# Row 0 of a two-layer graph kernel: a third transposed buffer, hand-over by blocks, products of zeros, constants prepared in pieces, and an epilogue product in three fp32r parts

## The chip, the cores and the metric

The kernel runs on one core of one Trainium2 chip. Its engines are TensorE (PE in the profile; its weight loads are PEld), VectorE (DVE), ScalarE (ACT), GpSimd (POOL) and SyncE (SP, which here only issues transfers). Sixteen DMA engines move data between HBM and the on-chip memory. The metric is the time of one execution in microseconds (us), lower is better.

## The reference

Two graph layers with a dense 6144 x 6144 matrix `adj` and features `x` of 6144 x 128, each followed by a residual and a normalisation. Cut to what matters:

```
x_norm = layernorm(x, g_in, b_in)
gate   = hard two-way choice from x_norm @ Wn + bn + gumbel(u)          # one number per node
view2  = (adj * gate[:, None] * gate[None, :]) @ x_norm
fg     = sigmoid(concat([x_norm, view2]) @ Wg + bg)
fused  = fg * (x_norm @ W1 + b1) + (1 - fg) * (view2 @ W2 + b2)
x      = layernorm(x + layernorm(fused + x, g_out, b_out))              # first layer
mv     = tanh(|x W^T| / |x| * artanh |x|) * (x W^T) / |x W^T|, clipped to a ball
xt     = logmap0(mobius_add(mv, expmap0(bias)))                         # features of the second layer
h      = expmap0(relu(logmap0(expmap0(adj @ xt))))                      # with clips to the ball
out    = layernorm(x + h)
```

## The kernel before

**Tiles.** Nodes are taken in 12 chunks of 512 (`NCH`, 4 blocks of 128, `BLK`). `adj` comes as 144 tiles of 1 MB, tile (c, q) being what output row c takes from chunk q. A tile n has two halves m = 2n and 2n + 1. A ring `A` holds five tiles. TensorE multiplies in fp32r, which keeps only part of the mantissa, so each half (128x1024) is split in two: ACT writes the high part (L565, `split_high`), DVE subtracts it from the half and writes the low part (L761, `split_low`), and PE makes three products for each of two blocks, high by high, low by high and high by low (L1023 to L1025). The places for split halves are four ring slots and some room in features not yet made (`XTH`, `XTL`), eight at this point.

**Row 0 is different.** Output row 0 (tiles 0 to 11) is summed while the features are made. PE multiplies the unsplit tile by unsplit features `FULL` in plain fp32 (L1021). For each chunk k, PE, ACT and DVE hand over in a ring: ACT `normalize` (L528, four blocks into `YB`), PE `transposes` (L1008), ACT `transposed` (L538, into one of two buffers `XNTB` = `XNT`, `X1T`, then a store to HBM by the ACT queue), PE `rows_and_logits` (L1015), DVE `gate_begin` (three small operations), ACT `gate_exp`, DVE `gate_end` (six small operations, L744 to L749), ACT `gated` (L550, four blocks into `FULL`), ACT `gated_high` (L556) and DVE `gated_low` (L753), which make the split features `XGH` and `XGL`. ACT's program is, for k = 0, 1, ...: `transposed(k+2)`, `gated(k+1)`, store of k+2, `normalize(k+3)`, `gated_high(k)`, load of block k+6 of x, `gate_exp(k+2)`. DVE's is: small step of k+3 (L719), `gate_end(k+1)`, `stats_pre(k+4)` (L710 to L716, which waits for block k+4 of x), `gate_begin(k+2)`, `gated_low(k)`. After its last `gated_low`, DVE runs `prepare()`: weights scaled, four bias vectors split in three bf16 terms (L766 to L777). ACT copies `RM` (L692) and only then begins to split tile 12.

**Epilogues.** Row c's sum is finished by an epilogue, front c, spread over the halves of the next row by tables: event e of row c + 1 is done after half 24(c + 1) + number, where the first number of a pair holds for the rows up to `LATE` = 6 and the second for later ones. For front 0, DVE's event "gate" (L853) stands after half 28, PE's "l0" (L1104 to L1112) after half 27. "gate" waits for three transfers that SP's `load_front` issues (`GB`, the gates for 512 nodes, `XNT` and `XR`; the semaphore `epi_in` counts all three). "l0" makes, for each of four blocks, a bias product, `XNT` by `RX` (256 columns, fp32, L1108), for the first fronts `XR` by the identity (L1110), and `GB` by `RS` (L1112). Then ACT takes tanh (L627), DVE fuses (L860 on) and normalises, with POOL for the powers. At the end SP stores the row (`store_x1`), and SP loads no tile meanwhile, as it runs in order.

**SP's order.** Tile n is loaded once tile n - 5 has been split (in row 0: used by PE). Before tile 16 stands the store of the gates to HBM, after `gate_rows` (L611 on ACT). Before tile 17 stands a wait for that store's landing, then `load_front(0)`.

Of the kernel before, what the change touches and what calls it, by code (L numbers as in the profile page):

```python
# [11 lines left out]
P = 128  # L12
BLK = 4
# [62 lines left out]
DVE_FIRST = {"m2m": (6, 1), "part": (7, 3), "gate": (4, 1), "q": (7, 1), "fuse": (10, 6), "stats1": (10, 8),  # L76
# [3 lines left out]
ACT_FIRST = {"mx": (3, 1), "tq": (9, 3), "tanh": (10, 6), "y1": (13, 11), "x1": (19, 15), "x1t": (19, 21),  # L80
# [28 lines left out]
def build(nc, x, adjT, u, w1, b1, w2, b2, wg, bg, wn, bn, g_in, b_in, g_out, b_out, w_hyp, b_hyp, out):  # L109
# [29 lines left out]
    with ExitStack() as ctx:  # L139
# [6 lines left out]
        FULL = sb("FULL", [P, 3, CW])  # L146
# [19 lines left out]
        RX = sb("RX", [P, 2 * P])  # L166
# [10 lines left out]
        BR = sb("BR", [P, CW], BF16)  # L177
# [5 lines left out]
        WH = PART[:, 1, 0:P]  # L183

# [34 lines left out]
        for name in (  # L219
# [4 lines left out]
                "xnt_stored0", "xnt_stored1", "epi_in",  # L224
                "hb_sq", "hb_norm", "hb_tanh", "hb_ready", "y2_ready", "rm_psum", "rm_ready", "wt_scaled", "bias_ready",
# [44 lines left out]
        XNTB = (XNT, X1T)  # L270
# [32 lines left out]
        def whole(q):  # L303
            return FULL[:, q % 3, :]

# [29 lines left out]
        def _(sp):  # L335
# [54 lines left out]
            for n in range(NCH + 3, NT):  # L390
# [4 lines left out]
                if n == 17:  # L395
                    sp.wait_ge(S["gate_stored"], 16)
                    sp.wait_ge(S["xnt_stored0"], 16 * (NCH // 2))
                    sp.wait_ge(S["xnt_stored1"], 16 * (NCH // 2))
                    load_front(0)
# [105 lines left out]
        def _(act):  # L505
# [18 lines left out]
            def normalize(k):  # L524
                act.wait_ge(S["pre_nm"], k + 1)
                wait_n(act, "pre_tr", k - 1)
                for t in range(BLK):
                    last = a.activation(YB[k % 2][:, blk(t)], XIN[k % 3][:, blk(t)], ACT.Identity,  # L528
                                        bias=NMP[:, k % 3, t:t + 1], scale=RSP[:, k % 3, t:t + 1])
                last.then_inc(S["pre_y"], 1)  # L530

            def transposed(k):
# [3 lines left out]
                wait_n(act, "pre_x", k - 1)  # L536
                wait_n(act, f"xnt_stored{k % 2}", 16 * (k // 2))
                a.activation(XNTB[k % 2][:, :], tbank(k), ACT.Identity, bias=BINC[:, 0:1],  # L538
# [6 lines left out]
            def gated(k):  # L545
# [3 lines left out]
                for t in range(BLK):  # L549
                    last = a.activation(whole(k)[:, blk(t)], xcell(k, t)[:, 0:P], ACT.Copy,  # L550
                                        scale=GATE[:, k * BLK + t:k * BLK + t + 1])
                last.then_inc(S["xgf"], 1)

            def gated_high(k):
                act.wait_ge(S["xgf"], k + 1)
# [147 lines left out]
        def _(dve):  # L703
# [23 lines left out]
            def neg_mean_pre(k):  # L727
                dve.wait_ge(S["pre_rs"], k + 1)
                wait_n(dve, "pre_y", k - 2)
# [454 lines left out]
```

## Time and profile before

| | us |
|---|---|
| median of three runs | 959.79 (958.04 to 961.10) |
| the profiled execution's own time | 959.55 |
| its span in the trace | 957.8 |
| PE busy | 911.9 (95%) |
| DVE busy | 788.0 (82%) |
| ACT busy | 680.3 (71%) |
| POOL busy | 232.4 (24%) |

The span is the stretch that the trace covers; 1.75 us of the execution's time lie around it. Busy time is the sum over an engine's instructions. PE's ends are modelled, and a matmul's busy time overlaps the next one's, so what a matmul costs in a row of them is read from start to start.

### The profile page before, as it was taken

The numbers are of one execution on the slowest core, as the hardware profiler recorded it, in microseconds if no ns is written. First come the engines' busy times: TensorE is split into PE (matmuls) and PEld (weight loads), VectorE is DVE, ScalarE is ACT, GpSimd is POOL, SyncE is SP. The second block draws the span as 40 slices with busy tenths as digits, with TensorE's granted clock in tenths as the row PEclk, the third lists the DMA queues.
The fourth block names the chain that finished last, engine by engine and source line by source line (L and its number), as shares of the span: only waits on it lengthen the run. The fifth ranks groups of instructions, "written<-read, shape, count | busy, mean of one in ns | idle before, by whom it ended". The sixth has DMA issues, their size and how long they took to land.

```text
span 957.8 us, 12537 instructions
## 1 busy us (share of the span) xinstructions
PE 911.9 (95%) x4032; PEld 720.3 (75%) x4032; DVE 788.0 (82%) x1781; ACT 680.3 (71%) x1214; POOL 232.4 (24%) x201
## 2 busy tenths in 40 slices
PE   4998998999999999999999999998999999999993
PEld 3555776777888878888888888886777878778772
DVE  3658899999989799879686775869899898989886
ACT  4786687878767576757566465666878989789873
POOL 2220212111111121101020010201100764485473
PEclk9999999999999999999999999999999999999997
DMA  7978596876949486958666584566799999999980
GB/s 264 358 282 314 224 424 250 327 316 254 380 192 386 185 350 224 346 190 284 232 253 230 177 304 179 216 258 229 275 355 363 410 375 408 371 402 394 419 333 33
DMA packets 51825, 281.72 MB, mean 294 GB/s; under 512 B 6528, under 2 KB 8496, under 8 KB 20656
## 3 DMA queue, kind: packets, MB, share of 16 engines
q1 hardware_dynamic: 46432, 271.48, 73.8%
q10 hardware_dynamic: 5328, 9.44, 2.8%
q8 instruction: 32, 0.52, 0.2%
q14 instruction: 33, 0.27, 0.1%
HBM read 271.44 MB, written 9.46 MB: 293 GB/s over the span
## 4 chain that ended last, share of the span: by engine, by line
PE 59%; DVE 24%; POOL 5%; ACT 5%; DMA 3%; issue 3%; POOLq 0%; DVEq 0%; SPq 0%; ACTq 0%
PE PS L1023 17%; PE PS L1025 17%; PE PS L1024 17%; DVE AL L761 5%; DVE XGL L761 4%; DVE XTL L761 3%; POOL r_rs L456 2%; PE PS L1112 2%; PE PS L1108 2%; DVE BS L710 2%; PE PS L1021 1%; DMA FU<-in_x_dram 1%; DMA A<-in_adjT_dram 1%; ACT FULL L550 1%; PE PS L1122 1%
## 5 line engine op out<-in xcount | busy, mean ns | idle before, releaser
L565 ACT ACTIVATE AH<-A 128x1024 fp32r<-128x1024 f32 x247 | 252.7, 1057 | 114.1 <-PE PS L1025 92.5
L761 DVE TENSOR_TENSOR AL<-A,AH 128x1024 fp32r<-128x1024 f32 x247 | 294.2, 1218 | 40.6 <-ACT AH L565 39.4
L1023 PE MATMUL PS<-AH,XGH 128*128 128x512 f32 x344 | 139.0, 404 | 4.0 <-DVE AL L761 4.0
L1025 PE MATMUL PS<-AH,XGL 128*128 128x512 f32 x344 | 134.2, 390 | 0.0
L761 DVE TENSOR_TENSOR XGL<-A,XGH 128x1024 fp32r<-128x1024 f32 x113 | 132.2, 1218 | 2.2 <-ACT XGH L565 2.0
L1024 PE MATMUL PS<-AL,XGH 128*128 128x512 f32 x344 | 134.0, 389 | 0.0
L565 ACT ACTIVATE XGH<-A 128x1024 fp32r<-128x1024 f32 x113 | 112.9, 1055 | 13.0 <-DMA A<-in_adjT_dram 11.4
L1023 PE MATMUL PS<-AH,XTH 128*128 128x512 f32 x290 | 114.8, 396 | 3.9 <-DVE AL L761 3.9
L1025 PE MATMUL PS<-AH,XTL 128*128 128x512 f32 x290 | 113.2, 390 | 0.0
L1024 PE MATMUL PS<-AL,XTH 128*128 128x512 f32 x290 | 113.0, 390 | 0.0
L456 POOL TENSOR_TENSOR r_rs<-r_v,NHALF 128x4 f32<-128x4 f32 x24 | 44.4, 1849 | 275.4 <-DVE r_v L716 275.4
L761 DVE TENSOR_TENSOR XTL<-A,XTH 128x1024 fp32r<-128x1024 f32 x92 | 108.5, 1218 | 0.1
L565 ACT ACTIVATE XTH<-A 128x1024 fp32r<-128x1024 f32 x92 | 93.2, 1051 | 6.9 <-DMA A<-in_adjT_dram 3.5
L1023 PE MATMUL PS<-XGH,XTH 128*128 128x512 f32 x226 | 91.3, 404 | 3.6 <-DVE XGL L761 3.6
L1025 PE MATMUL PS<-XGH,XTL 128*128 128x512 f32 x226 | 88.6, 392 | 0.0
L1024 PE MATMUL PS<-XGL,XTH 128*128 128x512 f32 x226 | 88.5, 392 | 0.0
L1023 PEld LDWEIGHTS PS<-AH,XGH 128*128 128x128 f32 x344 | 64.7, 188 | 18.6 <-DVE AL L761 4.3
L1023 PE MATMUL PS<-XTH,XGH 128*128 128x512 f32 x184 | 72.4, 394 | 4.4 <-DVE XTL L761 4.4
L1025 PEld LDWEIGHTS PS<-AH,XGL 128*128 128x128 f32 x344 | 64.6, 188 | 13.9
L1024 PEld LDWEIGHTS PS<-AL,XGH 128*128 128x128 f32 x344 | 64.7, 188 | 13.0
L1025 PE MATMUL PS<-XTH,XGL 128*128 128x512 f32 x184 | 72.3, 393 | 0.0
L1024 PE MATMUL PS<-XTL,XGH 128*128 128x512 f32 x184 | 72.3, 393 | 0.0
(245 smaller groups left out, 1560.2 us busy)
## 6 DMA issues: line engine op xcount, KB each, us to landing
A<-in_adjT_dram SPq DMA_DIRECT2D x243, 1024.0 KB, 7.1
GB<-gate_scratch SPq DMA_DIRECT2D x12, 256.0 KB, 3.6
XNT<-xnt_scratch SPq DMA_DIRECT2D x12, 256.0 KB, 4.0
XR<-in_x_dram SPq DMA_DIRECT2D x12, 256.0 KB, 4.8
x_scratch<-X SPq DMA_DIRECT2D x12, 256.0 KB, 7.7
xnt_scratch<-XNT ACTq DMA_DIRECT2D x6, 256.0 KB, 4.9
xnt_scratch<-X1T ACTq DMA_DIRECT2D x6, 256.0 KB, 3.9
XR<-in_x_dram ACTq DMA_DIRECT2D x4, 256.0 KB, 6.6
```

The lines of the kernel that those rows point to most:

```text
L456: g.tensor_tensor(dst, src, NHALF[:, 0:src.shape[-1]], ALU.pow).then_inc(S[done], 1)
L550: last = a.activation(whole(k)[:, blk(t)], xcell(k, t)[:, 0:P], ACT.Copy, scale=GATE[:, k * BLK + t:k * BLK + t + 1])
L565: a.activation(high(m), A[:, n % RING, h * HW:(h + 1) * HW], ACT.Copy).then_inc(S["hi"], 1)
L710: last = v.bn_stats(BS[:, t, :], src[:, blk(t)])
L761: v.tensor_tensor(low(m), A[:, n % RING, h * HW:(h + 1) * HW], high(m).bitcast(F32), ALU.subtract).then_inc(S["lo"], 1)
L1021: return p.matmul(acc, whole(q)[:, blk(t)], A[:, m // 2 % RING, t * CW:(t + 1) * CW], start=start, stop=stop)
L1023: p.matmul(acc, hi[:, st], high(m)[:, mv], start=start, stop=False)
L1024: p.matmul(acc, hi[:, st], low(m)[:, mv], start=False, stop=False)
L1025: return p.matmul(acc, lo[:, st], high(m)[:, mv], start=False, stop=stop)
L1108: p.matmul(E[:, t, 0:2 * P], XNT[:, blk(t)], RX[:, :], start=False, stop=False)
L1112: last = p.matmul(E[:, t, right], GB[:, blk(t)], RS[:, right], start=False, stop=True)
L1122: last = p.matmul(E[:, t, 0:P + 1], X1T[:, blk(t)], RM[:, :], start=True, stop=True)
```

## The change

Six things are changed.

1. A third buffer, `HY`, joins `XNTB`, with a third store semaphore; `transposed(k)` waits for what used the buffer three chunks ago instead of two.
2. Hand-over by blocks: `pre_y` and `xgf` are raised after each of the four blocks, PE's transposes and row 0's products wait for their own block.
3. Products of zeros: PE multiplies `ones` by the zeroed `BP` (bf16, 512 columns, into a bank that row 1 starts afresh), 16 times at the start and 3 times after each of the first four steps.
4. `prepare()` is cut in pieces, run in the loop over k at k = 6 to 10, between `stats_pre(k+4)` and `gate_begin(k+2)`. The copy of `RM` on ACT moves behind the second half of tile 12.
5. The product `XNT` by `RX` is made in three fp32r parts: `XNH` by `RXH`, `XNL` by `RXH`, `XNH` by `RXL`. For it ACT copies `XNT` to `XNH` (event "xnh": after half 24c + 2, later rows 24c + 0) and DVE subtracts (event "xnl": after half 24c + 3, later rows 24c + 0). For front 0 the copy also waits for the end of row 0, whose `FULL` it overlays. "xnh" waits for `epi_in`, and "l0" for `xnl`. `RX` is split once, in the last piece of the constants.
6. Room: `FULL`'s third buffer becomes `FULL2`; `XNH`, `XNL` and `RXL` lie on what row 0 leaves free.

```
-ACT_FIRST = {"mx": (3, 1), ...
+ACT_FIRST = {"xnh": (2, 0), "mx": (3, 1), ...
-DVE_FIRST = {"m2m": (6, 1), ...
+DVE_FIRST = {"xnl": (3, 0), "m2m": (6, 1), ...
-        XNTB = (XNT, X1T)
+        XNTB = (XNT, X1T, HY)
...
             def transposed(k):
                 act.wait_ge(S["pre_tr"], k + 1)
-                wait_n(act, "pre_x", k - 1)
-                wait_n(act, f"xnt_stored{k % 2}", 16 * (k // 2))
+                wait_n(act, "pre_x", k - 2)
+                wait_n(act, f"xnt_stored{k % 3}", 16 * (k // 3))
...
+                if event == "xnh" and front is not None:
+                    act.wait_ge(S["epi_in"], 48 * (front + 1))
+                    if front == 0:
+                        act.wait_ge(S["used"], 2 * NCH)
+                        act.wait_ge(S["xgl"], NCH)
+                    else:
+                        act.wait_ge(S["l0_mm"], front)
+                    a.activation(XNH[:, :], XNT[:, :], ACT.Copy).then_inc(S["xnh"], 1)
...
-            act.wait_ge(S["rm_psum"], 1)
-            a.activation(RM[:, :], PS[:, 4, 0:P + 1], ACT.Copy).then_inc(S["rm_ready"], 1)
...
+                if m == 2 * NCH + 1:
+                    act.wait_ge(S["rm_psum"], 1)
+                    a.activation(RM[:, :], PS[:, 4, 0:P + 1], ACT.Copy).then_inc(S["rm_ready"], 1)
...
+                if event == "xnl" and front is not None:
+                    dve.wait_ge(S["xnh"], front + 1)
+                    v.tensor_tensor(XNL[:, :], XNT[:, :], XNH[:, :].bitcast(F32), ALU.subtract).then_inc(S["xnl"], 1)
...
+            def keep_clock(count):
+                for _ in range(count):
+                    p.matmul(PS[:, 1, :], ones[:, :], BP[:, :], start=True, stop=True)
...
                 for t in range(BLK):
+                    pe.wait_ge(S["pre_y"], BLK * k + t + 1)
                     last = p.transpose(tbank(k)[:, blk(t)], YB[k % 2][:, blk(t)], ident)
...
                 for t in (2 * h, 2 * h + 1):
+                    if c == 0 and n < N2:
+                        pe.wait_ge(S["xgf"], BLK * q + t + 1)
...
+            pe.wait_ge(S["const"], 1)
+            keep_clock(16)
...
+                    pe.wait_ge(S["xnl"], front + 1)
...
-                        p.matmul(E[:, t, 0:2 * P], XNT[:, blk(t)], RX[:, :], start=False, stop=False)
+                        p.matmul(E[:, t, 0:2 * P], XNH[:, blk(t)], RXH[:, :], start=False, stop=False)
+                        p.matmul(E[:, t, 0:2 * P], XNL[:, blk(t)], RXH[:, :], start=False, stop=False)
+                        p.matmul(E[:, t, 0:2 * P], XNH[:, blk(t)], RXL[:, :], start=False, stop=False)
```

Where instructions move: ACT at the end of row 0 and the start of row 1. Before, `GATET`, then `RM`, then eleven splits in a row up to the tanh of front 0 (an instruction that writes `XTH` or `AH` from `A` is a split).

```order
L556 ACTIVATE XGH<-FULL 128x512 x2
L611 ACTIVATE GATET<-PS 48x128
L692 ACTIVATE RM<-PS 128x129
L565 ACTIVATE XTH<-A 128x1024 x4
L565 ACTIVATE AH<-A 128x1024 x4
```

The same place now:

```order
L559 ACTIVATE XGH<-FULL 128x512 x2
L614 ACTIVATE GATET<-PS 48x128
L568 ACTIVATE XTH<-A 128x1024 x2
L708 ACTIVATE RM<-PS 128x129
L568 ACTIVATE XTH<-A 128x1024
L625 ACTIVATE XNH<-XNT 128x512
L568 ACTIVATE XTH<-A 128x1024
L568 ACTIVATE AH<-A 128x1024 x4
```

`RM` has moved behind two splits, and `XNH` stands behind the third split of row 1, with all others behind it.

DVE at the same place. Before, the constants stand between the last low part of the features and the first low part of tile 12:

```order
L753 TENSOR_TENSOR XGL<-FULL,XGH 128x512 x2
L766 TENSOR_SCALAR RX<-RX 128x128
L767 TENSOR_SCALAR RS<-RS 128x128
L770 TENSOR_TENSOR PART<-PART 128x128
L771 TENSOR_SCALAR PART<-PART 128x128
L772 TENSOR_SCALAR PART<-PART 128x128
L774 CAST BP<-PART 1x512
L775 CAST BR<-PART 128x512
L776 TENSOR_TENSOR PART<-PART,BR 128x512
L774 CAST BP<-PART 1x512
...
L761 TENSOR_TENSOR XTL<-A,XTH 128x1024 x4
```

The same place now:

```order
L761 TENSOR_TENSOR GATE<-TOP,LG 128x4
L794 CAST BP<-PART 1x512
L795 CAST RXH<-PART 128x256
L796 TENSOR_TENSOR RXL<-PART,RXH 128x256
L765 TENSOR_TENSOR XGL<-FULL,XGH 128x512 x2
L773 TENSOR_TENSOR XTL<-A,XTH 128x1024 x4
L871 TENSOR_TENSOR XNL<-XNT,XNH 128x512
L773 TENSOR_TENSOR AL<-A,AH 128x1024
L875 TENSOR_TENSOR GB<-PS,GB 128x512
```

The low parts of row 1 follow the features at once, and `XNL` stands between the fourth and the fifth of them, ahead of the gate.

## Rows read from the trace of the kernel before

**Rows 1.** The page: the chain that ended last, by engine.

```profile
PE 59%; DVE 24%; POOL 5%; ACT 5%; DMA 3%; issue 3%; POOLq 0%; DVEq 0%; SPq 0%; ACTq 0%
```

**Rows 2.** Windows: stretch, length, PE, PEld, DVE, ACT, POOL busy; clock; DMA share, GB/s.

```profile
80.00:90.00 10.00, 6.42 (x21) 5.03 (x21) 9.07 (x12) 8.36 (x9) 0.00 (x0) 0.83 0.86 303
```

**Rows 3.** Timeline, one chunk of row 0: start, length, engine, line, what [idle before].

```profile
61.30 0.37 ACT L550 ACTIVATE FULL<-PS,GATE 128x128 f32<-128x128 f32 x1 [0.66 <-DVE GATE L749]
...
62.31 1.65 ACT L528 ACTIVATE TH<-FU,NMP,RSP 128x128 f32<-128x128 f32 x4
...
63.85 0.63 ACT L556 ACTIVATE XGH<-FULL 128x512 fp32r<-128x512 f32 x1
...
64.51 0.69 DVE L753 TENSOR_TENSOR XGL<-FULL,XGH 128x512 fp32r<-128x512 f32 x1 [1.31 <-ACT XGH L556]
...
65.19 0.16 DVE L744 TENSOR_TENSOR SM<-LG 128x4 f32<-128x4 f32 x1
...
66.39 0.37 ACT L550 ACTIVATE FULL<-PS,GATE 128x128 f32<-128x128 f32 x1 [0.66 <-DVE GATE L749]
...
67.58 0.30 PEld L1021 LDWEIGHTS PS<-A,FULL 128*128 128x128 f32 x2 [0.25 <-ACT FULL L550]
```

**Rows 4.** The start: a piece of the chain, then two rows of the timeline.

```profile
13.52 13.12 DMA FU<-in_x_dram
```

```profile
23.68 0.78 ACT L538 ACTIVATE XNT<-PS,BINC,GINC 128x512 f32<-128x512 f32 x1 [5.42 <-DMA xnt_scratch<-XNT]
...
26.66 0.87 DVE L710 BATCH_NORM_STATS2 BS<-FU 128x6 f32<-128x128 f32 x4 [6.94 <-DMA FU<-in_x_dram]
```

**Rows 5.** Timeline, from row 0 to row 1, ACT, DVE and PE.

```profile
76.98 0.27 ACT L611 ACTIVATE GATET<-PS 48x128 f32<-48x128 f32 x1
...
77.83 0.22 DVE L766 TENSOR_SCALAR RX<-RX 128x128 f32<-128x128 f32 x1
...
78.22 1.96 PE L1021 MATMUL PS<-A,FULL 128*128 128x512 f32 x4
...
78.57 3.88 ACT L565 ACTIVATE XTH<-A 128x1024 fp32r<-128x1024 f32 x4
...
82.39 4.63 DVE L761 TENSOR_TENSOR XTL<-A,XTH 128x1024 fp32r<-128x1024 f32 x4
...
83.76 0.47 PE L1023 MATMUL PS<-XTH,XGH 128*128 128x512 f32 x1 [3.58 <-DVE XTL L761]
...
87.44 0.43 PE L1023 MATMUL PS<-XTH,XGH 128*128 128x512 f32 x1
```

**Rows 6.** Timeline, the transfers that front 0 needs, and DVE's wait for them.

```profile
77.28 0.34 SPq L394 DMA_DIRECT2D gate_scratch<-GATET  x1
...
80.21 0.34 SPq L344 DMA_DIRECT2D A<-in_adjT_dram  x1
...
82.40 0.33 SPq L349 DMA_DIRECT2D GB<-gate_scratch  x1
...
88.94 0.69 DVE L853 TENSOR_TENSOR GB<-PS,GB 128x512 f32<-128x512 f32 x1 [0.78 <-DMA XR<-in_x_dram]
```

**Rows 7.** Timeline of PE: three starts at full clock, then one block of front 0.

```profile
89.10 0.40 PE L1024 MATMUL PS<-XTL,XGH 128*128 128x512 f32 x1
89.33 0.39 PE L1025 MATMUL PS<-XTH,XGL 128*128 128x512 f32 x1
...
91.10 0.59 PE L1108 MATMUL PS<-RX,XNT 128*128 128x256 f32 x2
91.53 0.38 PE L1110 MATMUL PS<-XR,IW 128*128 128x128 f32 x2
91.75 0.81 PE L1112 MATMUL PS<-RS,GB 128*128 128x384 f32 x2
```

**Rows 8.** The chain that ended last, from 175 to 210 us: start, length, what.

```profile
175.07 0.60 DVE GB L853
...
209.60 0.50 PE PS L1023
```

More of the change, by code:

```diff
@@ L75 @@
 CLOSE = 12
-DVE_FIRST = {"m2m": (6, 1), "part": (7, 3), "gate": (4, 1), "q": (7, 1), "fuse": (10, 6), "stats1": (10, 8),
+DVE_FIRST = {"xnl": (3, 0), "m2m": (6, 1), "part": (7, 3), "gate": (4, 1), "q": (7, 1), "fuse": (10, 6), "stats1": (10, 8),
              "nm1": (11, 9), "resid": (13, 9), "curv0": (14, 4), "affine": (13, 11), "stats2": (13, 11),
@@ L145, in build @@
         AL = sb("AL", [P, SPLITS, HW], F32R)
-        FULL = sb("FULL", [P, 3, CW])
+        with nc.sbuf_tensor("FULL", [P, 2, CW], F32) as FULL, nc.sbuf_tensor("BR", [P, CW], BF16) as BR:
+            pass
+        XNH = sb("XNH", [P, CW], F32R)
+        XNL = sb("XNL", [P, CW], F32R)
+        RXL = sb("RXL", [P, 2 * P], F32R)
+        FULL2 = sb("FULL2", [P, CW])
         XGH = sb("XGH", [P, N], F32R)
@@ L303, in whole @@
         def whole(q):
-            return FULL[:, q % 3, :]
+            return FULL2[:, :] if q % 3 == 2 else FULL[:, q % 3, :]
         def second_features(q):
@@ L396, in _ @@
                     sp.wait_ge(S["gate_stored"], 16)
-                    sp.wait_ge(S["xnt_stored0"], 16 * (NCH // 2))
-                    sp.wait_ge(S["xnt_stored1"], 16 * (NCH // 2))
+                    for i in range(3):
+                        sp.wait_ge(S[f"xnt_stored{i}"], 16 * (NCH // 3))
                     load_front(0)
@@ L527, in normalize @@
                 for t in range(BLK):
[L528 to L530 removed]
+                    a.activation(YB[k % 2][:, blk(t)], XIN[k % 3][:, blk(t)], ACT.Identity,
+                                 bias=NMP[:, k % 3, t:t + 1], scale=RSP[:, k % 3, t:t + 1]).then_inc(S["pre_y"], 1)
             def transposed(k):
@@ L549, in gated @@
                 for t in range(BLK):
-                    last = a.activation(whole(k)[:, blk(t)], xcell(k, t)[:, 0:P], ACT.Copy,
-                                        scale=GATE[:, k * BLK + t:k * BLK + t + 1])
-                last.then_inc(S["xgf"], 1)
+                    a.activation(whole(k)[:, blk(t)], xcell(k, t)[:, 0:P], ACT.Copy,
+                                 scale=GATE[:, k * BLK + t:k * BLK + t + 1]).then_inc(S["xgf"], 1)
             def gated_high(k):
-                act.wait_ge(S["xgf"], k + 1)
+                act.wait_ge(S["xgf"], BLK * (k + 1))
                 a.activation(XGH[:, xcols(k)], whole(k), ACT.Copy).then_inc(S["xgh"], 1)
@@ L805, in _ @@
                     stats_pre(k + 4)
+                prepare(k)
                 if k + 2 < NCH:
@@ L1012, in rows_and_logits @@
                 pe.wait_ge(S["pre_xt"], k + 1)
-                wait_n(pe, "xgf", k - 1)
+                wait_n(pe, "xgf", BLK * (k - 1))
                 for t in range(BLK):
-                    last = p.matmul(xcell(k, t), XNTB[k % 2][:, blk(t)], IW[:, :], start=True, stop=True)
+                    last = p.matmul(xcell(k, t), XNTB[k % 3][:, blk(t)], IW[:, :], start=True, stop=True)
                 last.then_inc(S["pre_x"], 1)
```

58 lines of the change are left out of this document (32 added, 26 removed).

## The prediction

> **What bounds the kernel now.** I read the page's chain first: PE holds 59% of the chain and DVE 24% [rows 1]. Whatever PE neither computes nor waits for is worth nothing, so the question for each edit is whether PE's start on something moves. Then I read three stretches in the timeline.
>
> In row 0 the reader is to see a ring of ACT and DVE that leaves PE out: `gated` starts at 61.30, `normalize` at 62.31, `gated_high` at 63.85, DVE's `gated_low` at 64.51, `gate_end` at 65.19, and the next `gated` at 66.39, 5.09 us after the last [rows 3]. PE waits 0.25 us for `FULL` in such a chunk [rows 3], so it is almost as slow, but the ring sets the pace.
>
> From row 0 to row 1, PE's last products of row 0 begin at 78.22 and last to about 80.2; it then idles 3.58 us until DVE, which spends 77.83 to 82.39 on constants, has the first low part, and starts at 83.76 [rows 5]. The granted clock of that stretch is 0.83 on average [rows 2]: nine products of row 1 run at the lower level (1.2 GHz), from 83.76 to 87.44, 0.41 us each [rows 5], where at the higher one they take 0.23 [rows 7].
>
> Front 0's inputs are the third: the gates are stored from 77.28, the loads wait for that store until 82.40, and DVE's gate starts only at 88.94, let go by the last of the three transfers [rows 6].
>
> **The change part by part.** *Third buffer.* ACT waited 5.42 us for the first store, until 23.68 [rows 4]; that wait goes. What is late next: DVE, in order, stands in `stats_pre(4)` until 26.66 for a block of x that was issued at 13.52 and took 13.12 us [rows 4], and `gate_end(2)`, without which ACT has nothing to go on with, is behind it. ACT issues that load after `gate_exp(0)`, at the same place of its program as before; a warmer PE lets it issue some tenths earlier, behind the same transfers. I take 0 for the start. Bounds: at most the 3 us from 23.68 to 26.66 if the transfer comes so much earlier, and 1 us lost, since PE now stands idle longer before 30 us, goes on at the lower clock, and has only 0.25 us a chunk in which to catch up. I add 0.2 for that.
>
> *Hand-over by blocks.* PE's 0.25 us of waiting a chunk go, but the ring of ACT and DVE has the same links of the same length; nothing comes of it until the last chunk, which no longer depends on the ring: 0.1 us. *Products of zeros.* They lie where PE waits for x and for ACT; 0.
>
> *Constants in pieces.* DVE has 1.31 us idle ahead of each `gated_low` [rows 3], and no `stats_pre` at k of 8 or more. The pieces last 0.4 to 1.6 us (4.56 us in all [rows 5], and the split of `RX`). They hide, but for about 0.5 us at k = 9 on the way to the last gates, which the hand-over by blocks covers for PE, not for the store of the gates. With them out of the way ACT splits from 77.3 (after `GATET` [rows 5]) and DVE from about 78.5, so PE could start row 1 at 80.2 instead of 83.76 and at the higher clock. Alone that is 3.6 us, and 9 x (0.41 - 0.23) = 1.6 us, 5.2 in all.
>
> *The new wait.* It isn't alone. ACT's `XNH` stands behind the third split of row 1 and waits for all three transfers of front 0. They land at 88.9 [rows 6]. Does the change bring them forward? Their loads start at the landing of the gates' store (82.40), whose issue at 77.28 follows `GATET` [rows 6], and `GATET` follows the last gates of the same ring; if anything it is later by up to 0.5 us. So ACT, having made splits 24, 25, 26 by 80.6, stands still until 88.9. Queued behind it are all further splits, behind those DVE and PE:
> - PE has three halves, 6 products of 0.23 us each: 80.2 + 4.1 = 84.3, then idle.
> - `XNH` is 128x512 on ACT, as `gated_high`: 0.6 us [rows 3]. Then split 27 on ACT (3.88 us for four, so 1.0 each [rows 5]), its low part on DVE (4.63 us for four, so 1.16 each [rows 5]) with 0.1 between: 88.9 + 0.6 + 1.0 + 0.1 + 1.2 = 91.8. PE has stood for 7.5 us, over the 3.58 after which the row showed the lower clock.
> - Half 27 at the lower level: 6 x 0.41 = 2.5, to 94.3. DVE meanwhile does `XNL` (as `gated_low`, 0.69 [rows 3]), low part 28 and the gate (0.69 [rows 6]), to 94.3. So l0 of front 0 starts at 94.3, before at about 91.0, a little ahead of its second product at 91.10 [rows 7]: 3.3 late. Its first 1.3 us still run at the lower clock: 0.6 more. Its `RX` part is shorter by 0.3 (below). Front 0's products are done 3.6 us later than before.
>
> From there on DVE is the chain, from the fusing of each front to the next gate, until 209.60 [rows 8]; a delay of front 0 is passed on whole, and the tile loads that wait for its end move with it. With up to 0.5 us for later gates I take +3.8 (3.0 to 4.5).
>
> *Cost of the parts on DVE and ACT.* A `XNL` of 0.7 and a `XNH` of 0.6 in each front. Front 1 falls into a stretch where ACT and DVE wait for tiles now and then: 0.4. Front 2's gate at 175.07 is inside the DVE chain [rows 8]: 0.7. Front 3 comes just behind that stretch: 0.2. Later rows are PE's, and DVE has room. Sum 1.3 (0 to 2.5).
>
> *The product.* Start to start, the fp32 product of 256 columns takes 91.53 - 91.10 = 0.43 us [rows 7]. Three fp32r products of 256 columns are not in the trace; of 512 columns one takes 89.33 - 89.10 = 0.23 [rows 7]. Half of that is 0.115, and a bit for what doesn't halve: 0.12, so 0.36 for three, and 0.07 saved for each block, 0.28 a front. Bounds: no less than 3 x 0.115; at most as long as the 512-column one if the weight load sets the pace, 0.69, a loss of 0.26 a block. Nearest is the 512-column row, which hides the same load; I keep to 0.12. It counts where PE is the chain, fronts 3 to 10: 8 x 0.28 = 2.2 gained (between 2.7 gained and 8.3 lost). That a load of 128 columns can be hidden under 256 columns is what the 128-column product makes likely: 91.75 - 91.53 = 0.22 us for two parts with a load each, 0.11 a part [rows 7].
>
> The Trainium skill (TensorE: Matmul & The Clock Gate, section LDWEIGHTS (loading the stationary operand)) gives a load of 128 columns as 128 / 1.2 = 107 ns, which is as long as 256 columns stream; by it, as an estimate, three parts take 0.32 to 0.33 us and the eight fronts give 3.3 us instead of 2.2. The trace has no such product to agree or disagree.
>
> **Sum.** Against the profiled execution's 959.55: start +0.2, last chunk -0.1, row 1 and front 0 +3.8, parts on DVE and ACT +1.3, product -2.2: +3.0, so 962.55. The median of the runs is 0.24 above the profiled execution: **962.8**. A measurement of this kernel can tell about 0.3% (2.9 us) from no change, that is 956.9 to 962.7, so my time stands right on the upper bound.
>
> **Rivals.**
> - *Faster: the start goes with the third buffer* (0.15). If block 4 of x lands up to 3 us earlier, as the same engines had other work queued then, all of row 0 moves, with the gates and front 0: 962.8 - 3 = 959.8; from there it is decided by the store of the gates: if that store of the gates no longer lands behind a tile, the 5.1 us to its landing (77.28 to 82.40 [rows 6]) shrinks by about 3, and ACT's stand with it: 956.8, and less with a shorter product. Against it: the load is at the same place in ACT's queue.
> - *The stall is there but is absorbed* (0.17): DVE's chain behind front 0 has slack that the rows don't show, for instance as it has fewer halves to split while it waits for tanh. Then front 0's delay counts by a half: 962.8 - 1.9 = about 961.
> - *The parts are slow* (0.10): three loads don't hide, 0.69 for 0.43. Eight fronts at 0.26 x 4 and the 2.2 not gained: 962.8 + 8.3 + 2.2 = 973 at the far end, 967 half way. The deciding point is a start to start of 0.143 us.
> - *The change does all it says* (0.05): the transfers of front 0 land before ACT needs them. 5.2 + 2.2 - 1.3: 953.7. The 88.94 speaks against it.
> - My forecast, the stall passed on whole: 0.53, spread from 961 to 965.5.
>
> The range of 8 in 10 is 956.0 to 967.0, which leaves out the case that does all it says and most of the slow parts. Faster by over 0.3%: half of the first rival and all of the fourth, 0.13. Slower: the slow parts and some 0.30 of my forecast, 0.40. Within: 0.23 of my forecast, the absorbed stall and the other half of the first rival, 0.47.
>
> **What would show it.** In the profile after: ACT idle before `XNH` by some 8 us, let go by the transfer of `XR`; PE idle some 7 us behind the third half of row 1, and nine or so products at half clock after it; front 0's gate at 94 instead of 88.94; start to start of the three parts at 0.12; `gated` every 5.09 us in row 0 as before; block 4 of x at 26 to 27. I am wrong if ACT has no such wait, if the ring's pace changes, or if block 4 lands well ahead of 26 us.

## The result, and the profile after

Times are medians in us over the runs of each kernel; the ratio is after over before, with its 95% interval.

| kernel | runs | median | lowest to highest | profiled execution | its span |
|---|---|---|---|---|---|
| before | 20 | 958.31 | 955.3 to 961.1 | 959.55 | 957.8 |
| after | 20 | 961.86 | 959.43 to 964.06 | 961.41 | 959.6 |

The ratio is 1.0037 [1.0029, 1.0045]: 3.55 us slower. (The first three runs of before had a median of 959.79; over twenty it is 958.31. The prediction's +3.0 was made against the profiled execution, so it is the difference that should be compared: +3.0 forecast, +3.55 measured.)

The page of the kernel after, its first part and its chain of work that ended last. Before, PE had 59% of the chain and DVE 24% [rows 1]:

```profile
PE 914.2 (95%) x4108; PEld 719.0 (75%) x4108; DVE 795.7 (83%) x1795; ACT 684.9 (71%) x1226; POOL 233.5 (24%) x201
...
PE 54%; DVE 28%; POOL 5%; DMA 4%; ACT 4%; issue 3%; POOLq 0%; SPq 0%; ACTq 0%; DVEq 0%
```

DVE has gained what PE lost: a longer part of the span is paced by DVE. Next the timeline of the kernel after from row 0 to front 0 (columns: start us, us busy, engine, line, operation, out<-in, shape, and in brackets the idle time before it and what ended it). First SyncE's queue, then ACT, DVE and PE; it answers to [rows 5 to 7].

```profile
76.69 0.34 SPq L399 DMA_DIRECT2D gate_scratch<-GATET  x1
82.11 0.33 SPq L354 DMA_DIRECT2D GB<-gate_scratch  x1
82.96 0.67 SPq L356 DMA_DIRECT2D XR<-in_x_dram  x1
...
76.40 0.27 ACT L614 ACTIVATE GATET<-PS 48x128 f32<-48x128 f32 x1
78.61 1.06 ACT L568 ACTIVATE XTH<-A 128x1024 fp32r<-128x1024 f32 x1
88.60 0.63 ACT L625 ACTIVATE XNH<-XNT 128x512 fp32r<-128x512 f32 x1 [8.93 <-DMA XR<-in_x_dram]
100.42 0.60 ACT L638 ACTIVATE TH<-PS 128x512 f32<-128x512 f32 x1 [3.61 <-PE PS L1148]
...
77.65 3.50 DVE L773 TENSOR_TENSOR XTL<-A,XTH 128x1024 fp32r<-128x1024 f32 x3 [0.32 <-ACT XTH L568]
90.21 1.23 DVE L773 TENSOR_TENSOR XTL<-A,XTH 128x1024 fp32r<-128x1024 f32 x1 [9.06 <-ACT XTH L568]
93.08 0.68 DVE L875 TENSOR_TENSOR GB<-PS,GB 128x512 f32<-128x512 f32 x1
...
79.02 0.47 PE L1048 MATMUL PS<-XTH,XGH 128*128 128x512 f32 x1 [0.16 <-DVE XTL L773]
91.49 0.79 PE L1048 MATMUL PS<-XTH,XGH 128*128 128x512 f32 x1 [8.11 <-DVE XTL L773]
94.22 0.54 PE L1141 MATMUL PS<-BP,ones 128*128 128x384 bf16 x1
```

PE gets into row 1 at 79.02, where before it started at 83.76 [rows 5], but after three halves it has nothing more: ACT stands for 8.93 us ahead of `XNH` until front 0's `XR` has landed, all further splits are queued behind it, DVE stands 9.06 us for the next split and PE 8.11 us for DVE's low part. Front 0's gate on DVE is at 93.08, before at 88.94 [rows 6]: 4.14 us late. PE starts the products of front 0 (l0) at 94.22, before at 90.93, and ACT's tanh of front 0, which the next steps hang on, comes at 100.42, before at 96.99: 3.43 us late. The rows of before:

```profile
90.93 0.34 PE L1107 MATMUL PS<-BP,ones 128*128 128x384 bf16 x1
...
96.99 0.60 ACT L627 ACTIVATE TH<-PS 128x512 f32<-128x512 f32 x1 [3.78 <-PE PS L1112]
```

Stretches of the kernel after (columns: window, its length, busy time and count of PE, of PE's loads, DVE, ACT, POOL, then granted clock, DMA share, GB/s):

```profile
80.00:90.00 10.00, 3.38 (x15) 2.44 (x13) 1.14 (x2) 1.40 (x2) 0.00 (x0) 0.92 0.85 288
90.00:100.00 10.00, 8.51 (x39) 6.41 (x39) 9.79 (x10) 6.81 (x8) 0.00 (x0) 0.74 0.69 249
```

Over this time DMA goes on at 85% and 69%, DVE and ACT have hardly anything in the first window and DVE is full in the second.

Where the loss comes from, by DVE's gate of each front (start in us, in one profile of each kernel):

| front | 0 | 1 | 2 | 3 | 4 | 5 | 6 | 8 | 10 | 11 | span |
|---|---|---|---|---|---|---|---|---|---|---|---|
| before | 88.94 | 130.92 | 174.99 | 219.07 | 263.15 | 310.59 | 358.44 | 465.21 | 582.86 | 645.95 | 957.8 |
| after | 93.08 | 134.83 | 179.50 | 224.16 | 268.83 | 314.95 | 362.18 | 468.29 | 585.28 | 648.05 | 959.6 |
| difference | 4.14 | 3.91 | 4.51 | 5.09 | 5.68 | 4.36 | 3.74 | 3.08 | 2.42 | 2.10 | 1.8 |

Three things are to be read off it: a delay of 4.1 us arises before front 0's gate (3.4 at its tanh); it grows by 0.6 us in each of the three steps from front 1 to front 4; from there 0.3 to 1.3 us a front come back. (These two profiles differ by 1.8 us, less than the medians do; block 4 of x, for which DVE waits at the start, landed 1.1 us earlier in the one of after, as told below.) The growth is `XNL`: from gate to gate it is 44.67, 44.66 and 44.67 us in after, 44.07, 44.08 and 44.08 in before, and in e2 below, which has no `XNL`, 44.07 in the last two of these steps.

### The profile page after: what moved, and what is told of

It is laid out like the page before. It is cut to its first block, busy times and chain, and to the rows that moved or that the text cites. A ratio compares the mean times of both kernels' runs of the same rounds, so it can differ in the third digit from the quotient of the medians.

```text
span 959.6 us, 12742 instructions
## 1 busy us (share of the span) xinstructions
PE 914.2 (95%) x4108; PEld 719.0 (75%) x4108; DVE 795.7 (83%) x1795; ACT 684.9 (71%) x1226; POOL 233.5 (24%) x201
## 4 chain that ended last, share of the span: by engine, by line
PE 54%; DVE 28%; POOL 5%; DMA 4%; ACT 4%; issue 3%; POOLq 0%; SPq 0%; ACTq 0%; DVEq 0%
PE PS L1048 16%; PE PS L1050 16%; PE PS L1049 16%; DVE AL L773 7%; DVE XTL L773 5%; DVE XGL L773 4%; POOL r_rs L461 3%; PE PS L1046 2%; DVE BS L722 2%; PE PS L1148 1%; DMA FU<-in_x_dram 1%; DMA A<-in_adjT_dram 1%; ACT FULL L554 1%; POOL r_minv L461 1%; ACT X L533 1%
## 5 line engine op out<-in xcount | busy, mean ns | idle before, releaser
L1050 PE MATMUL PS<-XGH,XTL 128*128 128x512 f32 x226 | 88.1, 390 | 0.0
L1049 PE MATMUL PS<-XGL,XTH 128*128 128x512 f32 x226 | 88.1, 390 | 0.0
```

Of the source, the lines that this page charges most:

```text
L1049: p.matmul(acc, hi[:, st], low(m)[:, mv], start=False, stop=False)
L1050: return p.matmul(acc, lo[:, st], high(m)[:, mv], start=False, stop=stop)
```

## The experiments

All kernels below compute the whole reference. The three groups of runs had medians of before of 958.9, 958.5 and 958.9, so only ratios are compared; 0.001 is about 1 us. e10 has five runs, e6 six, e11 seven and e12 eight, the others eleven or twelve. All profiles are of single executions, and one kernel's executions lie 2.5 to 6 us apart. Against before:

| kernel | ratio | interval |
|---|---|---|
| after | 1.0037 | 1.0029 to 1.0045 |
| e1: after, front 0's steps behind half 31 | 0.9993 | 0.9984 to 1.0002 |
| e2: after, product whole | 1.0005 | 0.9994 to 1.0017 |
| e3: before, parts alone | 1.0009 | 1.0000 to 1.0017 |
| e4: before, third buffer alone | 1.0001 | 0.9990 to 1.0012 |
| e5: after, constants in one go | 1.0009 | 0.9999 to 1.0019 |
| e6: after, no products of zeros | 1.0041 | 1.0028 to 1.0054 |
| e7: after, parts from front 5 on | 1.0002 | 0.9992 to 1.0011 |
| e8: e7, front 0's steps behind half 31 | 0.9993 | 0.9982 to 1.0004 |
| e9: e7, inputs of front 0 sooner | 1.0001 | 0.9992 to 1.0010 |
| e10: e9, zeros ahead of front 0 | 0.9959 | 0.9947 to 0.9972 |
| e11: after, zeros inside the stall | 1.0032 | 1.0021 to 1.0043 |
| e12: e9, front 0 two halves later | 0.9971 | 0.9960 to 0.9983 |

**Is it the wait of `XNH`?** e1 keeps every piece of work and moves the four events of front 0 (so far behind halves 26, 27, 28 and 27) behind half 31, so that five more splits stand ahead of the waiting instruction on ACT.

```
+FRONT0 = {"xnh": 7, "xnl": 7, "gate": 7, "l0": 7}
-                    out.setdefault(2 * NCH * c + after[c > LATE], []).append((event, c))
+                    at = FRONT0.get(event, after[0]) if c == 1 else after[c > LATE]
+                    out.setdefault(2 * NCH * c + at, []).append((event, c))
```

> The changed kernel, with front 0's four steps (XNH on ACT, XNL and the gate on DVE, l0 on PE) all placed behind half 31 of row 1, instead of behind 26, 27, 28 and 27. Nothing is computed otherwise. Theory (the wait of ACT for front 0's transfers is what loses the time): all eight places for split halves are filled before ACT waits, so ACT's wait of 8.93 us before XNH shrinks to 2 to 4 us, PE's 8.11 us of idle time in row 1 to under 1.5 us, no product of row 1 runs at the lower clock, front 0 is fused near 97.3 instead of 101.05, and the time is 3.5 to 5 us under the changed kernel's: 957 to 958.4, ratio to the kernel before 0.999 to 1.000. Rival (DVE paces rows 1 to 4 anyway and absorbs the stall): DVE's fuse moves, but the time stays at 961 to 962, ratio 1.003 to 1.004.

Measured: 0.9993, 4.2 us better than after. The timeline of e1:

```profile
89.08 0.63 ACT L627 ACTIVATE XNH<-XNT 128x512 fp32r<-128x512 f32 x1 [4.05 <-DMA XR<-in_x_dram]
91.40 0.32 PE L1143 MATMUL PS<-BP,ones 128*128 128x384 bf16 x1 [0.63 <-DVE GB L877]
97.77 0.69 DVE L884 SCALAR_TENSOR_TENSOR FU<-TH,PS 128x512 f32<-128x512 f32 x1 [3.33 <-ACT TH L640]
110.21 0.76 PE L1050 MATMUL PS<-AH,XGH 128*128 128x512 f32 x1 [2.93 <-DVE AL L775]
```

The transfer lands at about the same time (89.08, in after 88.60, in before 88.94), but ACT has only 4.05 us to wait and PE 0.63. Moving the steps removes the loss. It doesn't turn it into a gain: PE idles 2.93 us before 110.21 instead, when it waits for a low part that DVE makes late, and goes on at the lower clock. A later place alone is worth little: e8 against e7 below, which have no `XNH` there, is 0.9 us, within the noise.

**Is it the product in parts?** e2 is after with one fp32 product from `XNT` and `RX` again, without `XNH` and `XNL`; e3 is the opposite, before with the parts alone.

```
...
-                        p.matmul(E[:, t, 0:2 * P], XNH[:, blk(t)], RXH[:, :], start=False, stop=False)
-                        p.matmul(E[:, t, 0:2 * P], XNL[:, blk(t)], RXH[:, :], start=False, stop=False)
-                        p.matmul(E[:, t, 0:2 * P], XNH[:, blk(t)], RXL[:, :], start=False, stop=False)
+                        p.matmul(E[:, t, 0:2 * P], XNT[:, blk(t)], RX[:, :], start=False, stop=False)
```

> The changed kernel with the product XNT by RX whole again in fp32 (no XNH, XNL, RXH, RXL); buffer, blocks, zeros and pieces of constants stay. Theory: without XNH nothing on ACT waits for front 0's transfers, so its gate is at 88.7 instead of 93.08 and l0 follows at 89.4; DVE saves 0.7 us in each of rows 1 to 4, PE pays 0.32 us more in each of fronts 4 to 10. Sum against the changed kernel -4.4 - 1.7 + 2.3 = -3.8: about 958, ratio to before 0.998 to 1.001. Rival (the loss comes from the edits in row 0, not from the product's wait): ratio stays at 1.003 or more.

> The kernel before with the product in three fp32r parts alone (XNH behind half 26, XNL behind half 27, as in the change); two transposed buffers, no blocks, no zeros, constants in one piece, RM copied first. Theory (the wait in ACT's program belongs to the product): ACT waits some 7 us before XNH although constants come late, PE idles twice (3.6 us before row 1, some 5 us behind its third half), front 0's gate is at 93 to 93.5, and the time is the changed kernel's plus the 1.1 us that its start gained: +4 to +5.5 us, ratio 1.004 to 1.006. Rival (the parts are a gain by themselves and row 0's edits lose it): ratio 0.996 to 0.999.

Measured: e2 1.0005, so the parts cost after 3.1 us. e3 1.0009: alone they cost only 0.9 us, and the expectation of 1.004 or more is missed. The timeline of e3 (of its fastest execution) says why:

```profile
86.53 0.63 ACT L627 ACTIVATE XNH<-XNT 128x512 fp32r<-128x512 f32 x1 [6.19 <-DMA XR<-in_x_dram]
...
83.28 0.77 PE L1041 MATMUL PS<-XTH,XGH 128*128 128x512 f32 x1 [4.25 <-DVE XTL L774]
89.43 0.50 PE L1041 MATMUL PS<-XTH,XGH 128*128 128x512 f32 x1 [0.49 <-DVE XTL L774]
...
97.80 0.60 ACT L640 ACTIVATE TH<-PS 128x512 f32<-128x512 f32 x1 [3.06 <-PE PS L1133]
```

ACT's wait is there (6.19 us), but with the constants where they were, PE begins row 1 only at 83.28. The same three halves then reach almost to the end of the wait (0.49 us idle), and PE has only one long idle time, the 4.25 us before row 1. tanh of front 0 is at 97.80, in after at 100.42. Part of what I had put down to the parts belongs to the parts and the early start together.

e2 shows in turn that the early start brings nothing even where `XNH`'s wait is gone. The timeline of e2:

```profile
89.71 0.32 PE L1137 MATMUL PS<-BP,ones 128*128 128x384 bf16 x1 [3.95 <-DVE GB L872]
97.44 0.60 ACT L637 ACTIVATE TH<-PS 128x512 f32<-128x512 f32 x1 [5.20 <-PE PS L1142]
```

PE idles 3.95 us because the gate waits for the same transfers (88.77), and then needs 7.7 us from the start of front 0's l0 to tanh.

**The third buffer, the zeros, the pieces.** e4 is before with the third buffer alone, e6 is after with `keep_clock` making no products, e5 is after with the pieces of the constants in one go behind row 0.

```
-        XNTB = (XNT, X1T)
+        XNTB = (XNT, X1T, HY)
...
```

```
-                for _ in range(count):
+                for _ in range(0):
```

```
-                prepare(k)
...
+            for k in range(6, 11):
+                prepare(k)
```

> The kernel before with the third transposed buffer alone. Theory: ACT's wait of 5.4 us for the first store goes, block 4 of x is next and lands at 25.5 to 26.8 as in every run so far, nothing moves behind it: ratio 0.999 to 1.001. Rival (the buffer moves the start by 1 us or more): ratio under 0.9990, block 4's statistics before 25.4.

> The changed kernel without the products of zeros (31 of them), all else kept. Theory: the first transposes and rows run at the lower clock again, block 4 of x is issued some 0.8 us later but lands in the same span of 25.5 to 26.8, and the time stays within 0.5 us of the changed kernel's: ratio to before 1.003 to 1.004. Rival (the warm clock is worth the 1.1 us by which the changed kernel's row 0 ran ahead in the profile): 1 us or more above the changed kernel, ratio 1.005.

> The changed kernel with the constants prepared in one go behind row 0 again (RM's copy stays behind two splits). Theory (with ACT's wait in place the pieces bring nothing, and cost a little: they hold back the last gates and with them the store, and they let PE stand so long that the clock falls): row 1 starts near 83 instead of 79.0, GATET comes 0.5 us earlier, XNH with it, PE's second idle time shrinks from 8.1 to under 2 us, half 27 and front 0's first block run at the higher clock, and the time is 0.5 to 2 us under the changed kernel's: 960 to 961.4, ratio to before 1.001 to 1.003. Rival (the pieces are worth the 5.2 us that row 1's start shows): 966 to 967, ratio 1.008 or more.

Measured: e4 1.0001, e6 1.0041 where after has 1.0037; neither can be told from nothing. e5 1.0009: without the pieces 2.7 us are won back (give or take 1.3), more than the 0.5 to 2 I had expected. The timeline of e5:

```profile
86.35 0.63 ACT L625 ACTIVATE XNH<-XNT 128x512 fp32r<-128x512 f32 x1 [7.59 <-DMA XR<-in_x_dram]
...
82.94 0.77 PE L1049 MATMUL PS<-XTH,XGH 128*128 128x512 f32 x1 [4.93 <-DVE XTL L773]
...
97.62 0.60 ACT L638 ACTIVATE TH<-PS 128x512 f32<-128x512 f32 x1 [3.06 <-PE PS L1149]
```

It is the picture of e3: the constants fill the time in which nothing else could be done. The difference to after, 2.8 us at tanh, has three parts. `GATET` in after is at 76.40 and in e5 at 75.49: 0.9 later, of which some 0.6 are the pieces on the way to the last gates and the rest the landing of x. The way from `XNH` to tanh is 11.82 us in after and 11.27 in e5: 0.55. The rest, some 1.3 us, is that the three transfers landed 12.2 us behind `GATET` in after and 10.9 in e5: the wait for the gates' store ended 5.42 us after its issue in after (76.69 to 82.11) and 3.75 in e5 (75.78 to 79.53). Whether the pieces have a part in that isn't settled: over the profiles of all kernels that load front 0 in this order the distance is 10.7 (e3) to 12.3 (e4, which has no pieces), and it doesn't follow the store's time (e1 12.1 with 3.66, e11 11.5 with 5.14).

**Can the wait be avoided and the gain of the parts kept?** In the later, PE-bound part the parts should give 0.3 us a front. e7 makes the parts only from front 5 on; e8 has moreover front 0's gate and l0 behind half 31.

```
-                if event == "xnh" and front is not None:
+                if event == "xnh" and front is not None and front >= SPLIT_FROM:
...
-                    pe.wait_ge(S["xnl"], front + 1)
+                    if front >= SPLIT_FROM:
+                        pe.wait_ge(S["xnl"], front + 1 - SPLIT_FROM)
```

```
+FRONT0 = {"gate": 7, "l0": 7}
```

> The changed kernel with the product in three parts only from front 5 on, whole in fp32 for fronts 0 to 4 (no XNH and XNL there). Theory: as with the whole product in rows 1 to 5, where DVE sets the pace, and 0.32 us gained in each of fronts 5 to 10, where PE does: 1.9 us under the kernel with the whole product, about 956, ratio to before 0.996 to 0.999. Rival (what is shorter on PE there is taken back by DVE or by tiles): the same time as with the whole product, within 0.5 us.

> The changed kernel with the parts from front 5 on only, and front 0's gate and products four halves later, behind half 31; its inputs are loaded as before. Theory: as the kernel with all four steps four halves later (0.9993), less 0.7 us of DVE in each of fronts 0 to 4 (XNL) of which DVE's chain shows 2.5 to 3.5, plus 0.08 x 4 x 4 = 1.3 us of PE in fronts 1 to 4 where PE does not set the pace: 2 to 3 us under it, ratio to before 0.9965 to 0.9975. Rival (DVE has room there): the same as that kernel, 0.999 to 1.000.

Measured: 1.0002 and 0.9993, both at their rival's end. From the gate of front 5 to that of front 11 it is 332.82 us in e7 and 335.33 in e2, so the profiles show the parts' gain: 2.5 us over six fronts (332.8 to 333.1 in every kernel with the parts there, 335.3 or 335.4 in the three without). But the medians of the two differ by 0.2 us, and so do the profiled executions (959.06 and 959.13): e7 is 1.7 us ahead at front 11 (644.43 and 646.12), 0.8 at 763 us and not at all at 802 (802.38 and 802.28). The gain in the PE-bound part is shown; that it reaches the time isn't. e8 has PE idle 2.94 us before 109.40, as e1.

**Front 0's inputs sooner.** Of the three transfers only the gates (`GB`) need the gates' store. e9 is e7 with the loads of `XNT` and `XR` issued before the wait for that store.

```
+                    sp.dma_start(XNT[:, :], xnt_dram[0:P, :]).then_inc(S["epi_in"], 16)
+                    sp.dma_start(XR[:, :], x[0:P, :]).then_inc(S["epi_in"], 16)
                 if n == 17:
                     sp.wait_ge(S["gate_stored"], 16)
-                    for i in range(3):
-                        sp.wait_ge(S[f"xnt_stored{i}"], 16 * (NCH // 3))
-                    load_front(0)
+                    sp.dma_start(GB[:, :], gate_dram[0:1, :].partition_broadcast(P)).then_inc(S["epi_in"], 16)
```

> As the kernel whose product is in three parts from front 5 on; in addition SP loads XNT and XR of front 0 right behind the issue of the gates' store, and only GB waits for its landing. Theory (after ACT's wait is gone, front 0's transfers pace the gate of front 0): GB lands 1.0 to 2.0 us before XR did, the gate of front 0 is at 86 to 87 instead of 88.1, and the time is 1 to 2 us under that kernel's, 957 to 958, ratio to before 0.997 to 0.999. Rival (tile 16 now stands behind the two loads, and ACT waits for it): no gain, ratio 1.000 to 1.001.

Measured: 1.0001, a miss. The profile is of its slowest execution (961.56, the median is 958.5), so only its first rows are read:

```profile
89.77 0.38 PE L1145 MATMUL PS<-BP,ones 128*128 128x384 bf16 x1 [3.01 <-DVE GB L878]
91.21 1.49 PE L1155 MATMUL PS<-RS,GB 128*128 128x384 f32 x2
97.49 0.60 ACT L641 ACTIVATE TH<-PS 128x512 f32<-128x512 f32 x1 [5.20 <-PE PS L1155]
```

Measured from the first work on block 4 of x (27.62), DVE's gate comes after 61.2 us, in e7 (25.70) after 62.4, so 1.2 us are won, and they are still there at tanh (69.9 and 71.1). They are gone by the gate of front 3: from the gate of front 1 to that of front 3 it is 89.90 us in e9 and 88.81 in e7. The expectation's rival isn't refuted either: ACT waits 0.55 us for a tile before 87.00, which it doesn't do in e7. The rows showed something else, though. PE had stood for 3.01 us and made the first half of front 0's products at the lower level of its clock: 7.7 us from 89.77 to 97.49, as in e2 and e7. In before the same way, 90.93 to 96.99, is 6.1. That was the clue: each kernel in which PE had been idle for long before front 0's products (3.95 us in e2, 4.37 in e7, 3.01 in e9) paid 1.7 us there.

**The clock ahead of front 0.** e10 is e9 with 14 products of zeros, into a bank that isn't in use, just ahead of PE's wait for that gate; e12 is e9 with l0 two halves later and the gate one, both behind half 29, so that twelve products of row 1 lie there instead. e11 puts 34 products of zeros into after's stall, ahead of half 27.

```
+                    if front == 0:
+                        keep_clock(14, 3)
                     pe.wait_ge(S["s1_gated"], front + 1)
```

```
+FRONT0 = {"gate": 5, "l0": 5}
```

```
+                    if m == 2 * NCH + 3:
+                        keep_clock(34, 3)
                     if m // 2 not in AHEAD.values():
```

> The kernel with the parts from front 5 on and front 0's inputs loaded earlier, with 14 products of zeros (3.0 us) on PE between half 27 and front 0's products, where PE stood idle 3.0 us and then ran its first two blocks at half clock (gate at 88.82, tanh only at 97.49). Theory: the products run at the higher clock, 5.6 us instead of 7.7; tanh comes 6.6 us behind the gate instead of 8.7; 1.5 to 2.1 us under the kernel without them: 956.4 to 957, ratio to before 0.998 to 0.9985. Rival (rows 1 to 4 are paced by tiles, not by front 0): tanh moves and the time doesn't, ratio 0.9995 to 1.0005.

> The kernel with the parts from front 5 on and front 0's inputs loaded earlier, with front 0's gate and products two halves later, behind half 29. Theory: PE makes two more halves (2.7 us) in the time in which it stood idle 3.0 us, keeps the higher clock, and starts front 0's products within 0.5 us of the same time; tanh 2 us earlier, and two halves more are done: 2 to 3 us under the kernel without it: 955.5 to 956.5, ratio to before 0.997 to 0.998. Rival (DVE's chain paces rows 1 to 4, two more halves done on PE are worth nothing): only the 1.5 to 2 us of the clock, ratio 0.998 to 0.9985, and PE idle before half 34 or later.

> The changed kernel with 34 products of zeros (into a bank not in use) ahead of half 27 of row 1, where PE stands idle 8.1 us; at 0.22 us each they fill 7.4 us of it. Nothing waits for them. Theory (part of the loss is the clock: half 27 and the start of front 0's products run at half clock behind the idle time): half 27 takes 1.4 instead of 2.7 us, the first block of front 0's products 1.4 instead of 1.8, the tanh of front 0 comes at 11.82 - 1.7 = 10.1 us behind XNH, and the time is 1.2 to 2 us under the changed kernel's: ratio to before 1.0015 to 1.0025. Rival (the gate of front 0 on DVE is late anyway, so that PE only waits elsewhere): tanh moves by under 0.7 us, ratio 1.003 or more.

Measured: e10 0.9959, e12 0.9971, e11 1.0032. The timeline of e10 (a row with `x13` is of zeros; the fourteenth isn't in the trace):

```profile
85.12 2.97 PE L1030 MATMUL PS<-BP,ones 128*128 128x512 bf16 x13
88.55 0.34 PE L1147 MATMUL PS<-BP,ones 128*128 128x384 bf16 x1 [0.47 <-DVE GB L878]
89.38 0.81 PE L1157 MATMUL PS<-RS,GB 128*128 128x384 f32 x2
94.61 0.60 ACT L641 ACTIVATE TH<-PS 128x512 f32<-128x512 f32 x1 [3.32 <-PE PS L1157]
```

The zeros take PE from 85.12 to 88.1, PE idles 0.47 us, and l0 runs at the higher level: 6.1 us from 88.55 to tanh instead of 7.7, and the two products with `RS` last 0.81 instead of 1.49. Two kernels that differ by these 14 products and nothing else are 0.4% apart (e9 1.0001, e10 0.9959, intervals clear of each other), and e10 is the fastest kernel of this study, 3.9 us (0.41%) under before. That is more than I had expected (0.998 to 0.9985) and more than the clock explains: it gives 1.7 us up to tanh. In the two profiles a further 1.4 us fall between the gates of front 1 and front 3 (88.51 us in e10, 89.90 in e9), where e9's ACT waits longer for a tile (4.43 us before 161.16, in e10 2.99 before 157.03) and for PE (2.19 us before the tanh of front 2, in e10 0.58). Whether that comes of the zeros or is scatter, as e7's 88.81 suggests, isn't shown, and e10 has only five runs. In e12 real products do the same service (6.05 us from l0 to tanh), but PE idles again later and falls to the lower clock (0.63 long, 0.43 from start to start):

```profile
107.81 0.75 PE L1053 MATMUL PS<-AH,XGH 128*128 128x512 f32 x1 [2.15 <-DVE AL L778]
108.36 0.63 PE L1054 MATMUL PS<-AL,XGH 128*128 128x512 f32 x1
```

It ends 1.2 us behind e10, with intervals that overlap.

In after the zeros do little. The stretch and the row of e11:

```profile
80.00:90.00 10.00, 9.93 (x45) 5.87 (x46) 1.97 (x2) 1.80 (x3) 0.00 (x0) 1.00 0.76 292
...
94.24 0.32 PE L1141 MATMUL PS<-BP,ones 128*128 128x384 bf16 x1 [0.99 <-DVE GB L875]
```

The clock is 1.00, half 27 is done by 93.1 and so a good 1 us sooner, and then PE waits 0.99 us for the gate, since DVE has to make `XNL`, low part 28 and the gate first. From `XNH` to tanh it is 11.27 us, in after 11.82: of after's stall the lower clock costs only 0.55 us, and the rest is the wait and what DVE does behind it. The rival is what happened (tanh moved by under 0.7, ratio 1.003 or more).

## Why the prediction was right, and which sizes were off

The time was forecast at 962.8 and is 961.86, and the difference at +3.0 where it is +3.55. The mechanism is the one forecast, and e1 shows it. That the sum is so close is partly luck: two terms were wrong by more than that, in opposite directions. In the two profiles, up to `GATET` after is 0.58 us ahead (76.40 and 76.98; forecast +0.1 for the start and the last chunk); from `GATET` to the tanh of front 0 it loses 4.0 (forecast +3.8); from there to the gate of front 4 another 2.25 (forecast +1.3); and to front 11 it wins back 3.6 (forecast -2.2). The last 0.3 us come back behind that. Step by step:

- **The wait of `XNH`, passed on whole (+3.8 forecast).** The likeliest case, and what happened: ACT idle 8.93 us, forecast "some 8"; PE idle 8.11, forecast about 7; l0 of front 0 starts 3.29 us late, forecast 3.3, and its tanh comes 3.43 late, forecast 3.6 for the products. e1 moves the wait and the loss is gone. The step was composed a little wrongly: DVE reached the gate at 93.08, not 93.6, and PE paid the clock over the 6 products of half 27 at 0.43 and more, as forecast, but e11 shows that DVE's `XNL`, low part and gate would have held l0 back to about the same time.
- **Constants in pieces (0 beside the stall, 5.2 gained alone).** Here I was off. The pieces aren't neutral beside the stall: after is 2.7 us slower than e5, give or take 1.3. In the profiles 0.6 of that is the delay of the last gates, and 0.55 the lower clock behind an idle time of PE that is long because row 1 began early and had nothing to go on with; the rest is open. And "5.2 alone" isn't there either: e2 has them without `XNH`, and is at 1.0005. I had overlooked what comes next: front 0's gate, and the tanh behind it, hang on the transfers and not on how soon PE begins row 1.
- **The parts on DVE and ACT (+1.3).** Too small. The forecast let DVE's stretch end at 209.60 [rows 8]; the gates grow apart by 0.6 us a front up to front 4 at 268.83, so the `XNL` of a front (0.68 us) counts almost in full three times, 1.8 us, and with the step from the tanh of front 0 to the gate of front 1 it is 2.25.
- **The product (-2.2).** The price of a block was right, the total too small. The timeline of one block of a later front in the kernel after:

```profile
419.13 0.28 PE L1138 MATMUL PS<-BP,ones 128*128 128x256 bf16 x1
...
419.48 0.28 PE L1143 MATMUL PS<-RXH,XNL 128*128 128x256 f32 x1
419.59 0.28 PE L1144 MATMUL PS<-RXL,XNH 128*128 128x256 f32 x1
419.71 0.59 PE L1148 MATMUL PS<-RS,GB 128*128 128x256 f32 x2
420.14 0.27 PE L1138 MATMUL PS<-BP,ones 128*128 128x256 bf16 x1
```

  And of front 7 before:

```profile
415.70 0.28 PE L1104 MATMUL PS<-BP,ones 128*128 128x256 bf16 x1
...
416.79 0.27 PE L1104 MATMUL PS<-BP,ones 128*128 128x256 bf16 x1
```

  From part to part it is 0.11 and 0.12 us, forecast 0.12; a block takes 1.01 us and before took 1.09, 0.08 saved where 0.07 was forecast. From front 4 to front 11 the difference of the gates falls from 5.68 to 2.10, 3.6 us. Of this 1.3 comes in the single step from front 4 to front 5. There PE paces before: its front 4 has DVE wait 1.49 us for the tanh, and after's has no such wait, so that a part of DVE's delay isn't passed on. The six steps behind it give 2.3, 0.38 a front, a little over the 0.32 of four blocks. The rival of slow parts (from 0.143 up) is refuted. The Trainium skill (TensorE: Matmul & The Clock Gate, section LDWEIGHTS (loading the stationary operand)) gives 107 ns for the load of 128 columns. The spacing of 0.11 and 0.12 agrees with a load that is just hidden, though the load records themselves last 0.19 us here; and the estimate from it, 3.3 us for eight fronts or 0.41 each, is nearer to the 0.38 measured than my 0.28.

- **Third buffer and start (+0.2).** Nothing measurable (e4 1.0001). In after's profile block 4 was worked on from 25.52, under the 26 that I had named as a sign against me. Yet over the fourteen profiles this time is 25.2 to 27.6 whatever the edit: e4 25.3, e6 26.5, e9 27.6, before 26.66 [rows 4]. It is a scatter between executions, and one profile couldn't have shown a shift of 1 us either way. (e4's 25.3 is the sign that its expectation named for its rival; with the ratio at 1.0001 it is the same scatter.)

The last two rows of the start, in after:

```profile
12.56 0.34 ACTq L516 DMA_DIRECT2D FU<-in_x_dram  x1
...
25.52 0.87 DVE L722 BATCH_NORM_STATS2 BS<-FU 128x6 f32<-128x128 f32 x4 [4.68 <-DMA FU<-in_x_dram]
```

  ACT issues the load 1.0 us sooner than before (13.52 [rows 4]) and DVE still waits 4.68 us for it: what the buffer frees, this transfer takes. The sooner issue isn't the buffer's (e4, with it alone, issues at 13.40, and e6, without the zeros, at 13.39).

- **Ring of row 0.** As forecast: `gated` starts at 60.34 and again at 65.44, 5.10 us apart, before 5.09 [rows 3].

What stays open: 1 to 1.5 us of the 2.7 that the pieces cost, which lie in where the transfers of front 0 land; why e7 isn't faster than e2, when its lead of 1.7 us is lost between 735 and 802 us, where the two run the same instructions; and some 2 us of e10's gain.

## What to carry to other kernels

An instruction that waits for a transfer must not stand in an in-order engine ahead of work that others live on; before adding one, read when its transfer lands and how much is queued behind it, and move it by that many steps (here five more splits ahead of it took all of the 4 us away). Work that is moved out of an engine's idle time gains nothing if the next link waits for something else, so read that next link first. And where a group that begins the critical chain comes just after PE has been idle, cheap products right ahead of its wait can be worth more than bringing the group forward (e10 against e9: 0.4%); the same products ahead of a group that waits for another engine anyway bring nothing that can be measured (e11).

## What the runs showed of the hardware

- After 3.0 to 4.4 us of idle time PE's next group began or soon went on at the lower level of its clock: front 0's products took 7.7 us to tanh in e2, e7 and e9, and 6.1 in e10, where products of zeros in bf16 had filled most of that time. The length of the idle time alone doesn't tell: in e12 2.15 us were followed by products at the lower level, in e8 2.94 us by six at the higher one (0.23 from start to start from 109.71), and in after's stall the granted clock was 1.00 up to 88 us, 4.6 us into it. Zeros count as work for the clock: the granted clock of 80 to 90 us is 0.92 in after and 1.00 in e11.
- A 24 KB store of the gates, issued at 76.69, let the loads that wait for it go at 82.11, 5.4 us later; over the profiles this took 3.4 to 5.4 us, and a load of 256 KB issued at 12.6 to 13.5 took 12 to 15. So I couldn't place such transfers to better than 1 or 2 us, which is as much as most of the edits here were worth.
- fp32r products of 256 columns with a new stationary operand each follow one another every 0.11 to 0.12 us, half of the 0.23 for 512 columns [rows 7].
